# Attention scores of one layer: the position bias moved from a VectorE pass into a four-row matmul

## The reference

```python
xn = layernorm(x)
q = (xn @ Wq).reshape(B, S, 32, 128);  k, v = split(xn @ Wkv)      # one k and one v head for all
scores = einsum("bqhd,bkd->bhqk", q, k) * 128 ** -0.5
rel = pos[None, :] - pos[:, None]                                   # key position - query position
scores = where(causal, scores + slopes[:, None, None] * rel, -inf)  # one slope per head
attn = softmax(scores) @ v
s = attn.reshape(B, S, 4096) @ Wo
g = silu(xn @ dequantised_w.T)                                      # int weights, groups of 128
x = x + s * g
...
```

## Time and profile before

| what | value |
|---|---|
| time of four runs, us | 9830.22, 9881.18, 10029.64, 10068.07; median 9955.41 |
| the profiled execution's own time | 9792.09 us |
| its span on the slowest core (core 7) | 9790.5 us |
| spans of all cores | 9685.9 to 9790.5 us |
| stage C in the span | 1595 to about 4780 us |
| head 0; heads 1 to 15; heads 16 to 30 | 77.7 us; 1649.7 us; 1280.2 us |

### The profile page before, as it was taken

How to read it: one execution, slowest core, us unless ns; L and a number is a source line. 1 busy time by engine, 2 the same in 40 slices (tenths; PEclk the granted TensorE clock), 3 DMA queues, 4 the chain that set the end, 5 groups by cost and what they waited for, 6 DMA issues and landing times.

```text
span 9790.5 us, 75559 instructions; the slowest of 8 cores (9685.9 to 9790.5 us)
## 1 busy us (share of the span) xinstructions
PE 5860.8 (60%) x24764; PEld 2280.8 (23%) x24764; DVE 2190.7 (22%) x3449; ACT 1706.8 (17%) x2284; POOL 268.7 (3%) x283
## 2 busy tenths in 40 slices
PE   0269795444443555555496987868402555488588
PEld 0124342001100111111143433333201222133233
DVE  5000002454445433333100001111331111111111
ACT  2000001333332444444100000000110100000000
POOL 0001010000000000000000000000000000000000
PEclk9789897666666666666698998989755988789899
DMA  6398885222222100000345448677642122567676
GB/s 211 73 91 90 101 90 91 63 84 60 60 65 81 32 13 13 13 13 11 74 110 108 113 117 160 153 165 160 181 145 69 40 70 70 113 132 152 136 154 135
DMA packets 1325213, 933.28 MB, mean 95 GB/s; under 512 B 984365, under 2 KB 1135949, under 8 KB 1316450
## 3 DMA queue, kind: packets, MB, share of 16 engines
q0 software_dynamic: 439472, 374.57, 23.0%
q1 hardware_dynamic: 848498, 503.53, 20.5%
q10 hardware_dynamic: 36864, 50.35, 1.6%
HBM read 730.14 MB, written 234.90 MB: 99 GB/s over the span
## 4 chain that ended last, share of the span: by engine, by line
PE 34%; DMA 22%; DVE 15%; SPq 11%; ACT 10%; issue 6%; another core or an unknown queue 1%; DVEq 1%; ACTq 0%; POOL 0%; POOLq 0%
PE B2ps L255 9%; DMA Gxb<-X 8%; PE B1ps L314 6%; DMA Dxb<-x 6%; PE CpsAV L610 4%; PE CpsL L619 4%; ACT Cptil L589 4%; DMA B1w<-wq 3%; PE FpsAV L804 3%; PE FpsS L853 3%; DVE CsbR L584 3%; SPq L226 2%; DMA WDQ<-B0wdq 2%; SPq L174 2%; SPq L713 2%
## 5 line engine op out<-in xcount | busy, mean ns | idle before, releaser
L255 PE MATMUL Gps<-Gw,GxnT 128*128 128x512 bf16 x4096 | 937.9, 389 | 309.3 <-DMA GxnT<-XN 188.7
L577 PE MATMUL CpsS<-Cq,kT_res 128*128 128x512 bf16 (+3 forms) x1280 | 479.9, 478 | 1038.5 <-DVE CsbR L584 1033.3
L1333 PE MATMUL Dps<-Dw,DxnT 128*128 128x512 bf16 x4096 | 914.1, 386 | 227.1 <-DMA Dw<-wo 142.6
L314 PE MATMUL B1ps<-B1xnT,B1w 128*128 128x512 bf16 x4096 | 899.0, 381 | 189.0 <-DMA B1xnT<-XN 149.2
L255 PE MATMUL B2ps<-B2w,B2xnT 128*128 128x512 bf16 x4096 | 887.6, 380 | 185.0 <-DMA B2w<-WDQ 185.0
L584 DVE SCALAR_TENSOR_TENSOR CsbR<-Crel,CpsS 128x1024 f32<-128x1024 f32 (+7 forms) x768 | 699.0, 910 | 915.7 <-ACT Clf L626 368.0
L589 ACT ACTIVATE Cptil<-CsbR,Chsc 128x1024 bf16<-128x1024 f32 (+7 forms) x768 | 690.5, 899 | 1033.2 <-DVE CsbR L584 991.5
L610 PE MATMUL CpsAV<-Cptil,Cvth 128*128 128x512 bf16 (+3 forms) x1280 | 560.9, 438 | 89.3 <-DVE Catn L642 85.6
L255 PEld LDWEIGHTS Gps<-Gw,GxnT 128*128 128x128 bf16 x4096 | 398.8, 100 | 819.3 <-issue 384.5
L1333 PEld LDWEIGHTS Dps<-Dw,DxnT 128*128 128x128 bf16 x4096 | 403.0, 99 | 738.2 <-issue 279.9
L314 PEld LDWEIGHTS B1ps<-B1xnT,B1w 128*128 128x128 bf16 x4096 | 402.2, 98 | 685.5 <-issue 220.6
(11 more groups left out here) (170 smaller groups left out, 3244.3 us busy)
## 6 DMA issues: line engine op xcount, KB each, us to landing
B1w<-wq POOLq DMA_DIRECT2D x64, 1024.0 KB, 13.9
B0cvt<-wqq POOLq DMA_DIRECT2D x128, 512.0 KB, 5.9
Dw<-wo POOLq DMA_DIRECT2D x16, 4096.0 KB, 34.9
Gw<-wbT POOLq DMA_DIRECT2D x16, 4096.0 KB, 33.7
Ax<-x POOLq DMA_DIRECT2D x16, 2048.0 KB, 12.5
WDQ<-B0wdq SPq DMA_DIRECT2D x128, 256.0 KB, 4.4
G<-B2ob ACTq DMA_DIRECT2D x128, 256.0 KB, 2.6
Dgb<-G SPq DMA_DIRECT2D x128, 256.0 KB, 3.5
```

Of the source, the lines that this page charges most:

```text
L255: p.step("tensor", lambda t, c=c, tt=tt, par=par, b=b, last=last: t.matmul(ps[b][:], xnT[:, c * TH + tt * 128: c * TH + (tt + 1) * 128], w ...
L314: p.step("tensor", lambda t, k=k, tb=tb, par=par, o=o, tw=tw: t.matmul(ps[2 * (o % 2) + tb][:, 0:tw], wsl[par][:, k * 128:(k + 1) * 128], ...
L577: h2=h2, hp=hp: t.matmul(psS[sl][:, qp0 - h2 * 1024: qp0 - h2 * 1024 + n], kT[:, kt * 128:(kt + 1) * 128], qbuf[hp][:, qg:qg + n], start=T ...
L1333: p.step("tensor", lambda t, c=c, tt=tt, par=par, b=b: t.matmul(ps[b][:], xnT[:, c * TH + tt * 128: c * TH + (tt + 1) * 128], wsl[par][:, ...
```

## The change

The bias and the mask are added by TensorE inside the PSUM accumulation, and VectorE's pass over the scores is gone. The scores are cut into tiles of up to 512 columns in four PSUM buffers instead of slabs of up to 1024 in two, so a head has 40 exponentials instead of 24, and each reads PSUM. For each tile a second matmul with 4 rows (Cprow, 4x128, against Ckrow4h, 4 rows of positions times the head's slope) is added (L589 of the new kernel), and for the first tile of each key tile a third one of 128 columns (L594), an identity product that adds the mask. Ckrow4h is made once per head by a new VectorE step (L508, 4x2048) at the head of the preparation, which waits for TensorE's work of the head before and on which ScalarE's L512 (the former L504) then waits. The 1 MB table Crel is no longer loaded; three small tables are.

A block of the second half is now emitted whole by `emit_av_qb`, behind key tiles 3, 7, 11 and 15, and the broadcast matmul (L641) stands right behind the denominator. The copies of the denominator (L635) and of the broadcast reciprocal (L644) move from ScalarE to VectorE.

```diff
-    rel_t = sb("Crel", [128, 2048], F32)
-    sbR = [sb(f"CsbR{i}", [128, 1024], F32) for i in range(2)]
+    prow4_b = sb("Cprow4", [4, 128], BF16)
+    krow4f = sb("Ckrow4f", [4, 2048], F32)
+    krow4h = [sb(f"Ckrow4h{i}", [4, 2048], BF16) for i in range(2)]
+    cmaskT_b = sb("CcmaskT", [128, 128], BF16)
...
-    psS = [psa(f"CpsS{i}", [128, 1024]) for i in range(2)]
+    psS = [psa(f"CpsS{i}", [128, 512]) for i in range(4)]
...
+        p.step("vector", lambda v, hp=hp, h=h: v.tensor_scalar(
+            krow4h[hp][:], krow4f[:], float(slopes[h]), None, OP.mult),
+            wait=[(SP, st[h - 1]["p1_pe"])] if h >= 1 else [])
+        krow_ms[hp] = SV.cur
...
-                        wait=([(DQT[hp], d_q), (SV, slab_stt[sl])]
-                              if j == 0 else []))
+                p.step("tensor", lambda t, kt=kt, sl=sl, n=n, qg=qg: t.matmul(
+                    psS[sl][:, 0:n],
+                    kT[:, kt * 128:(kt + 1) * 128],
+                    qbuf[hp][:, qg:qg + n], start=True, stop=False),
+                    wait=[(DQT[hp], d_q), (SS, slab_exp[sl]),
+                          (SV, krow_ms[hp])])
+                p.step("tensor", lambda t, kt=kt, sl=sl, n=n, qp0=qp0,
+                       hp=hp, diag=diag: t.matmul(
+                    psS[sl][:, 0:n],
+                    prow4_b[:], krow4h[hp][:, qp0:qp0 + n],
+                    start=False, stop=not diag))
+                if diag:
+                    p.step("tensor", lambda t, sl=sl: t.matmul(
+                        psS[sl][:, 0:128], cmaskT_b[:], ident_b[:],
+                        start=False, stop=True))
                 mm = SP.cur
-                p.step("vector", lambda v, sl=sl, hl=hl, h2=h2, h=h: v.scalar_tensor_tensor(
-                    sbR[sl][:, 0:hl], rel_t[:, h2 * 1024:h2 * 1024 + hl],
-                    float(slopes[h]), psS[sl][:, 0:hl], OP.mult, OP.add),
-                    wait=[(SP, mm), (SS, slab_exp[sl])])
...
+                    psS[sl][:, 0:n], AF.Exp, bias=hsc[hp][:, 8 + kt:9 + kt]),
...
         av_ms = SP.cur
+        lcp = p.step("vector", lambda v, bs=bs: v.tensor_copy(
+            lf[0:1, 0:bs], psL[0:1, 0:bs]), wait=[(SP, av_ms)])
-        p.step("scalar", lambda sc, bs=bs: sc.activation(
-            lf[0:1, 0:bs], psL[0:1, 0:bs], AF.Copy), wait=[(SP, av_ms)])
...
-        rbc = p.step("scalar", lambda sc, bs=bs: sc.activation(
-            rb[:, 0:bs], psR[:, 0:bs], AF.Copy), wait=[(SP, rbm)])
+        rbc = p.step("vector", lambda v, bs=bs: v.tensor_copy(
+            rb[:, 0:bs], psR[:, 0:bs]), wait=[(SP, rbm)])
...
+        emit_pass1(h, interleave=(
+            (lambda kt, h=h: emit_av_qb(h - 1, kt // ktg)
+             if (h >= 1 and kt % ktg == ktg - 1 and kt // ktg < nqb) else None)))
```

More of the change, by code:

```diff
@@ L464, in _phase_att0 @@
     psQ = psa("CpsQ", [128, 512])
-    p.dma("gpsimd", lambda g: g.dma_start(out=rel_t[:], in_=dram["rel"][:, :]), DCC)
+    p.dma("gpsimd", lambda g: g.dma_start(out=prow4_b[:], in_=dram["prow4"][:, :]), DCC)
+    p.dma("gpsimd", lambda g: g.dma_start(out=krow4f[:], in_=dram["krow4"][:, :]), DCC)
+    p.dma("gpsimd", lambda g: g.dma_start(out=cmaskT_b[:], in_=dram["cmaskT"][:, :]), DCC)
     d_cc = DCC.cur
@@ L493, in _phase_att0 @@
            wait=[(DKN2, d_kn2)])
-    slab_exp = [0, 0]
-    slab_stt = [0, 0]
+    slab_exp = [0, 0, 0, 0]
+    krow_ms = [0, 0]
     half_ctr = 0
@@ L565, in emit_pass1 @@
             L = T - kt * 128
-            nhalf = (L + 1023) // 1024
-            for h2 in range(nhalf):
-                sl = half_ctr % 2
+            nq4 = (L + 511) // 512
+            for h2 in range(nq4):
+                sl = half_ctr % 4
                 half_ctr += 1
[L570 to L580, removed]
-                        wait=([(DQT[hp], d_q), (SV, slab_stt[sl])]
-                              if j == 0 else []))
-                mm = SP.cur
-                p.step("vector", lambda v, sl=sl, hl=hl, h2=h2, h=h: v.scalar_tensor_tensor(
-                    sbR[sl][:, 0:hl], rel_t[:, h2 * 1024:h2 * 1024 + hl],
-                    float(slopes[h]), psS[sl][:, 0:hl], OP.mult, OP.add),
-                    wait=[(SP, mm), (SS, slab_exp[sl])])
[L588 to L593, removed]
@@ new lines, in emit_pass1 @@
+                n = min(512, L - h2 * 512)
+                qp0 = h2 * 512
+                qg = kt * 128 + qp0
+                diag = (h2 == 0)
+                p.step("tensor", lambda t, kt=kt, sl=sl, n=n, qg=qg: t.matmul(
[9 more added lines that the diff above has]
+                    start=False, stop=not diag))
@@ new lines, in emit_pass1 @@
+                if diag:
+                    p.step("tensor", lambda t, sl=sl: t.matmul(
+                        psS[sl][:, 0:128], cmaskT_b[:], ident_b[:],
+                        start=False, stop=True))
+                mm = SP.cur
+                p.step("scalar", lambda sc, kt=kt, sl=sl, n=n, h2=h2, hp=hp: sc.activation(
+                    ptil[hp][:, off[kt] + h2 * 512: off[kt] + h2 * 512 + n],
+                    psS[sl][:, 0:n], AF.Exp, bias=hsc[hp][:, 8 + kt:9 + kt]),
+                    wait=([(SP, mm), (SV, st[h]["bneg"])]
+                          if (kt == 0 and h2 == 0) else [(SP, mm)]))
@@ L598, in emit_pass1, with emit_av_qb @@
         st[h]["exp_all"] = SS.cur
-    def emit_av_mm(h, qb):
+    def emit_av_qb(h, qb):
         hp = h % 2
@@ L649, in emit_av_fin @@
                 DAS[hp], wait=[(SV, SV.cur)])
[L651 to L669 removed]
+    ktg = max(1, nkt // max(1, nqb))
     for h in range(32):
@@ L679, in _phase_att0 @@
             interleave()
-        emit_pass1(h, interleave=pump)
-        drain_actions()
-        actions["q"] = [("mm", h, qb, None) for qb in range(nqb)]
-    drain_actions()
+        emit_pass1(h, interleave=(
+            (lambda kt, h=h: emit_av_qb(h - 1, kt // ktg)
+             if (h >= 1 and kt % ktg == ktg - 1 and kt // ktg < nqb) else None)))
+    for qb in range(nqb):
+        emit_av_qb(31, qb)
     return [DQT[0], DQT[1], DAS[0], DAS[1], DKN, DKN2]
```

27 lines of the change are left out of this document (3 added, 24 removed).

## The result

The changed kernel takes 10269.0 us (median of 7 runs, 10117.77 to 10454.32) against 9984.19 us for the kernel before beside it (10 runs). The ratio of the executions in which neither die ran markedly slower than the other is 1.0267 (the two medians, of all executions, give 1.0285), 95% interval 1.0164 to 1.0371: **slower**, though the interval leaves open whether by more than 2%. I had forecast a ratio of 0.985. What came true is the slow rival, "the bias matmul does not hold the clock", which stood at +2.2%.

A forecast was written before the change was run, and what follows sets the result against it. No engine is busy over 60% of the span, so each stage has its own limit. Light heads 16 x 2.4, heavy 15 x -10.1, head 0 -24, start -5 sum to -143 us, ratio 0.985, 9810 us; range 9660 to 10150.

The forecast's parts named there:

- the slow rival: Score stretches stay at 1.2 GHz with the 4-row bias matmul: light head 100.2 us, +214 us in all, 10174 us; chance 0.18.
- After each pause I charge PE 3.5 us at 1.2 GHz: In score stretches and value blocks, PE was taken to run 3.5 us at 1.2 GHz after each wait, then 2.4.
- 0.63 us for score plus bias: Price on PE of a 512-column score matmul with its bias matmul: 0.63 us at 2.4 GHz, 1.06 at 1.2.
- One sum of chances: Chance that the changed kernel is faster by over 2%, summed as 0.10 + 0.13 + 0.03 = 0.27.
- The preparation: Start of each head, from ScalarE's square until the first exponential can start: 21.5 us, unchanged by the edit.
- The pause: Four times a head PE waits behind the denominator for copy, logarithm and exponential before the broadcast: 2.5 us each.
- The exponential of 512 columns from PSUM: ScalarE's price for one full score tile: 0.690 us, 0.78 with the idle time between steps.
- The tail: End of a head, with nothing beside it: broadcast, copy, product, scaling of the position rows and gaps, 3.5 us.
- The copy behind the dequantisation: In a heavy head the first denominator's copy queues on VectorE until 24.7 us, ready at 12.5: 12.2 us more.
- that rival: PE's clock survives the 2.5 us pauses: light heads 2.3 us less, heavy 14.3 less, 9667 us in all; chance 0.16.
- The start: Start of the stage, where ScalarE waits 17.7 us for the 1 MB table: 5 us less, bounds 0 and 17.7.
- The loads: Rival: the bias matmul's weights load unseen, a pair costs 0.43 us, 238 us less, 9713 us in all; chance 0.04.

## Why the prediction was wrong

**The step that failed** is the clock: "After each pause I charge PE 3.5 us at 1.2 GHz", with 0.63 us for score plus bias behind it. I took the 3.5 us from a block of value and one-column matmuls and carried them to stretches in which every second matmul has 4 rows. Those stretches never rose from 1.2 GHz (11.80 us of full work at 0.50), so a pair cost 1.07 us, not 0.63. With 128 rows and one column, where the price of 0.63 us does hold, the forecast's heads nearly come out: 88.76 us for 87.7, 102.7 for 99.9, head 0 49.1 for 54. So the sum was sound in the main and its premise was not. Some of that agreement is luck: in that kernel's light head at 4163 the clock came back 4.9, 6.2 and 6.5 us behind the first three broadcasts, not 3.5. One sum of chances is off by a hundredth (0.10 + 0.13 + 0.03 is 0.26, not 0.27), which changes nothing. I had used "those blocks are half one-column matmuls and rise all the same" as evidence against the slow rival. It was none: the one-column matmuls use 128 rows, the bias matmul 4, and columns and rows of the weights are not the same thing to the clock.

**The slow rival** had it right with 0.18 of the chances: 102.35 for 100.2, heavy 110.8 for 109.8, head 0 58.3 for 61.7. Its missing 2 us a light head are in the blocks: from the first broadcast to the second it is 21.9 us (4378.30 to 4400.23), where its terms give 20.6. In the head shown, block 0 (3.0 us) never leaves 1.2 GHz, and blocks 1 to 3 rise 6.1, 5.6 and 4.0 us in, where I took 3.5.

**What held.** The preparation: 21.46 us from the square to the first exponential (21.5). The pause: 2.50 us four times a head (2.5). The exponential of 512 columns from PSUM: 0.688 us (0.690). The tail: 3.56 us (3.5), with 1.215 us for the scaling of the position rows (1.2 to 1.3). Pair of score and bias at 1.2 GHz: 1.07 us (1.06). Mask matmul: 0.08 us (0.05 to 0.17). The copy behind the dequantisation: 8.5 us (12.2), and as a wait of PE at most 14.1 us. The clock does not survive a pause of 2.5 us: in light heads blocks 1 to 3 end at 2.4 GHz, and each of these 45 times the clock was at 1.2 GHz 2.1 to 3.2 us behind the block's last matmul. With 128 rows and one column of weights it fell behind every pause too (1.5 to 4.2 us), so it is not the 4 rows alone; that rival is out. The start gained 17.7 - 14.9 = 2.8 us, not 5.

**The loads.** The Trainium skill, "TensorE: Matmul & The Clock Gate", step-by-step part, has the next weights pulled in under the running matmul. The runs agree for 128 x 128 and 128 x 96 weights (0.43 us from start to start at 1.2 GHz and 0.22 at 2.4, by columns alone). They do not for 4, 32 and 64 rows or one column in turn with 128 x 128 (0.52 to 0.54 us at 1.2 GHz; 0.31 to 0.32 at 2.4 with one column, which few-row pairs never reached). Here it was worth 3 to 5 us a light head, the lesser part.

Why the chip treats few rows so is not shown by these runs; that it does, with 4, 32 and 64 rows alike, is.

## What to carry to other kernels

Before moving an elementwise pass to TensorE as a matmul of a few rows, look at the granted clock of the stretch that it would join: such a matmul fills PE's time without bringing its clock up. Padding the operands with zero rows to 128 cost PE nothing here (it was busy for 817 us instead of 1081 in 15 light heads) and gave back 17 us of 102. The order of the work is worth as much: scores between a block and its broadcast gave back 14 us of a light head with 4 rows, and both together 25. And a step that frees an engine is worth only what its list lets through: 17 us a heavy head came from spreading the dequantisation, with no new arithmetic.
